# The loop over images of a Mamba layer, written out

## The chip, the cores and the metric

The kernel runs on one core of a Trainium2 chip. The metric is the device time in microseconds of one execution, taken as the median of several runs. All data is fp32.

## The reference

Two layers work on an input of 8 images, 384 channels, 32 x 32 positions. Each is `x = x + layer(groupnorm(x))`. The first layer is a Mamba block over the 1024 positions of an image, and an MLP:

```
t  = layernorm(tokens)                          # 8 x 1024 x 384
xm, z = split(t @ in_proj_w.T)                  # 768 channels each
xc = silu(causal_conv3(xm) + conv_b)
dt, B, C = split(xc @ x_proj_w.T)               # 24, 16, 16
dt = softplus(dt @ dt_proj_w.T + dt_proj_b)
h[l]  = exp(dt[l] * A) * h[l-1] + dt[l] * xc[l] * B[l]   # 768 channels x 16 states
y  = (sum over the states of h * C + xc * D) * silu(z)
t  = gelu(y @ out_proj_w.T @ mlp_w1.T + mlp_b1) @ mlp_w2.T + mlp_b2
```

The second layer routes each position to two of four experts, each a two-layer perceptron of 384 channels, and adds them up.

## The kernel before, in words

The kernel has four blocks: a set-up (weights, group statistics), the Mamba layer, a gate stage, and the experts. In each block every engine has its own stream of instructions, and the streams are held together by semaphores alone.

The Mamba layer works in *units*: half an image, 512 positions with the channels on the 128 partitions, so 16 units. A unit goes through three phases:

- *pre*: group norm and layer norm, in-projection (MU, VAR, XM), convolution, the projections to dt, B and C (XP, CT, DT);
- *scan*: 32 *slots*, one for each of 16 states and each of two groups of three channel blocks. In a slot GpSimd forms the input product `vv` (L475), ScalarE three exponentials (L485), VectorE three scans along the positions (L513); TensorE transposes the result (L544), and VectorE multiplies it by C and adds it to `yy` in four instructions (L531, or L529 in the first two slots);
- *post*: transposes of `yy` (Y, L583), the skip term on VectorE (L590), z (Z, L601), out-projection (O, L639), the MLP (M1, L663; M2, L694), the residual on VectorE (L705, L710) and the statistics for the next layer's norm (L714).

The function `step` writes a *half step*: the scan of one unit, with the post phase of the unit before it and the pre phase of the unit after it. The order of the dense work is written out by hand (`ORDER`, with pads and lags in slots), and shared out over the slots of the scan; VectorE takes at most two dense operations behind each scan. `program` calls `step` for all units. Two half steps (the second half of an image, the first half of the next) are the body of a hardware loop, `eng.Fori(0, NB - 1)` at L1089, of seven iterations. Every engine runs that loop by itself, with a counter in a register, and branches back at its end. One half step without post phase stands before it, one without pre phase behind it.

Waits go through the class `Event`: L111 is its `wait_ge`. A unit's number `unit.n` is `b * 2 + half`; inside the loop `b` is the loop's register, so the value waited for has to be computed by register operations at run time:

```
        eng.wait_ge(self.sem, unit.n * (self.per_unit * self.step)
                    + (self.base + (i + 1 - back * self.per_unit) * self.step))
```

With a plain number it is a constant, and a wait that reaches back before the first unit is left out (`unit.static and unit.n < back`). In the same way tiles and DRAM tensors indexed by the image (`st1` at L714, `gn0` at L725, the loads and stores of `x`) have an address from a register in the loop and a constant one outside. The experts' block has a loop of its own over images (L1533), and the gate stage some small ones.

Of the kernel before, what the change touches and what calls it, by code (L numbers as in the profile page):

```python
# [26 lines left out]
NB, C, L = 8, 384, 1024  # L27
# [212 lines left out]
def layer0(nc, a, sem, psum, ident, st1, gn0, eps, x_d, x1_d, b_d, dt, wu, vv, consts):  # L240
    with ExitStack() as ctx:
# [306 lines left out]
        def exp_table(eng):  # L548

            eng.preload_act_table_set("natural_log_exp_and_others")  # L550
# [533 lines left out]
        def program(eng, name):  # L1084
            if name == "act":
                exp_table(eng)
            step(eng, name, pres=Unit(0, 0))
            step(eng, name, scan=Unit(0, 0), pres=Unit(0, 1))
            with eng.Fori(0, NB - 1) as i:  # L1089
                step(eng, name, scan=Unit(i, 1), posts=Unit(i, 0), pres=Unit(i + 1, 0))  # L1090
                step(eng, name, scan=Unit(i + 1, 0), posts=Unit(i, 1), pres=Unit(i + 1, 1))
            step(eng, name, scan=Unit(NB - 1, 1), posts=Unit(NB - 1, 0))
            step(eng, name, posts=Unit(NB - 1, 1))

        s_const = sem("layer1_constants")
        with nc.Block() as block:
            @block.sync
            def _(eng):
                for event in (e_m1, e_m2, e_bn, e_st, e_yz, e_sz, e_t, e_ge, e_x1):
                    event.prime(eng)  # L1100
                program(eng, "sync")
                e_st.wait(eng, Unit(NB - 1, 1))

            @block.gpsimd
            def _(eng):
                program(eng, "pool")
                last = Unit(NB - 1, 1)
                e_v.wait(eng, last)
                e_scan.wait(eng, last)
                for tile, src in consts.loads:  # L1110
                    eng.dma_start(tile, src).then_inc(s_const, 16)
                eng.wait_ge(s_const, 16 * len(consts.loads))

            @block.scalar
            def _(eng):
                program(eng, "act")

            @block.vector
            def _(eng):
                program(eng, "dve")  # L1120

            @block.tensor
            def _(eng):
                program(eng, "pe")
# [499 lines left out]
```

## Time and profile before

| | us |
|---|---|
| median of 3 runs (4445.4 to 4457.47) | 4446.55 |
| profiled execution: its own time | 4449.6 |
| profiled execution: span | 4447.9 |
| VectorE busy in the span | 3558.9 |
| TensorE busy in the span | 3895.6 |
| ScalarE busy in the span | 2557.5 |
| GpSimd busy in the span | 2453.9 |

The span runs from the first to the last instruction of the profiled execution. The engines' streams overlap, so busy times don't add up. A row of the timeline gives start, duration, engine, line and operation, and in brackets the idle time of the engine before it with what ended it; "issue" is idle time in which the engine waited for nothing that the profile shows. Rows of engines with a q behind the name are instructions that the engine's sequencer handles itself, such as branches, register operations and waits.

### The profile page before, as it was taken

How to read it: one execution, taken by the hardware profiler on the slowest of the kernel's cores; microseconds unless marked ns; L12 is line 12 of the kernel's file. 1: busy time of each engine (PE TensorE's matmuls, PEld its weight loads, DVE VectorE, ACT ScalarE, POOL GpSimd, SP SyncE). 2: the span in 40 equal slices, each digit the busy share in tenths (PEclk: the TensorE clock that was granted, in tenths of full speed). 3: DMA queues.
4: the chain of work that ended last, by engine and by line, in shares of the span. 5: the costliest groups of instructions: out<-in, count | busy, mean ns of one | idle time of the engine just before them, and what ended most of it. 6: DMA issues, size and time to landing. Idle time of an engine off the chain costs nothing. (4 is left out here: it accounts for less than half of the span.)

```text
span 4447.9 us, 55651 instructions
## 1 busy us (share of the span) xinstructions
PE 3895.6 (88%) x15209; PEld 2309.2 (52%) x15209; DVE 3558.9 (80%) x4770; ACT 2557.5 (57%) x3970; POOL 2453.9 (55%) x1172
## 2 busy tenths in 40 slices
PE   4568998989898989888998889898978959999999
PEld 3234444444444444444444444444444438888887
DVE  3699998999899999989998999899998245556554
ACT  2466666666676757676666666676754323434343
POOL 1686777777667777776777777767775110000000
PEclk9679999999999999999999999999989969999999
DMA  4011211121111111221211121111111241112110
GB/s 161 31 40 38 68 46 58 47 68 50 58 52 52 52 59 45 69 66 38 68 47 57 47 68 45 61 54 52 52 49 47 105 145 38 38 38 57 38 38 34
DMA packets 114427, 252.94 MB, mean 57 GB/s; under 512 B 11324, under 2 KB 11708, under 8 KB 113636
## 3 DMA queue, kind: packets, MB, share of 16 engines
q1 hardware_dynamic: 108176, 227.12, 15.4%
q0 software_dynamic: 3920, 17.98, 1.1%
q10 hardware_dynamic: 2052, 4.52, 0.3%
q8 instruction: 127, 2.08, 0.2%
q14 instruction: 152, 1.25, 0.1%
HBM read 223.82 MB, written 25.76 MB: 56 GB/s over the span
## 5 line engine op out<-in xcount | busy, mean ns | idle before, releaser
L475 POOL TENSOR_TENSOR vv<-wu,bb 128x1536 f32<-128x1536 f32 x512 | 1767.0, 3453 | 922.1 <-DVE hh L513 920.4
L485 ACT ACTIVATE bank<-dt,a_neg 128x512 f32<-128x512 f32 x1536 | 1046.4, 689 | 1092.4 <-DVE hh L513 1061.9
L544 PEld LDWEIGHTS bank<-ident,hh 128*128 128x128 f32 x6144 | 783.5, 150 | 1208.3 <-DVE yy L531 520.7
L544 PE MATMUL bank<-ident,hh 128*128 128x128 f32 x6144 | 1067.8, 299 | 306.8 <-DVE yy L531 276.6
L531 DVE SCALAR_TENSOR_TENSOR yy<-bank,ct,yy 128x384 f32<-128x384 f32 x1920 | 1110.9, 597 | 55.2 <-PE bank L544 53.2
L513 DVE TENSOR_TENSOR_SCAN hh<-bank,hl,vv 128x512 f32<-128x512 f32 x768 | 978.6, 1274 | 113.8 <-ACT bank L485 84.2
L513 DVE TENSOR_TENSOR_SCAN hh<-bank,vv 128x512 f32<-128x512 f32 x768 | 930.4, 1212 | 127.8 <-ACT bank L485 94.7
L663 PE MATMUL bank<-tt,wring 128*128 128x512 f32 x1152 | 555.8, 598 | 24.4 <-ACT hid L678 19.9
L694 PE MATMUL bank<-hid,wring 128*128 128x512 f32 x1152 | 550.3, 595 | 7.9 <-ACT hid L678 6.1
L1527 POOL DMA_DIRECT2D out<-xb x16 | 12.3, 766 | 839.3 <-DVE xb L1522 839.3
L1477 ACT ACTIVATE dt<-bank,vv 128x512 f32<-128x512 f32 x192 | 132.2, 689 | 387.0 <-PE bank L1398 386.9
L792 PE MATMUL bank<-xn,w_in 128*128 128x512 f32 x576 | 299.4, 631 | 38.6 <-POOL xn L782 38.4
L639 PE MATMUL bank<-xc,w_out 128*128 128x512 f32 x576 | 293.2, 627 | 0.0
L1496 DVE TENSOR_TENSOR dt<-dt,wu 128x512 f32<-128x512 f32 x192 | 129.7, 689 | 191.5 <-ACT dt L1477 191.5
L601 PE MATMUL bank<-xn,w_in 128*128 128x512 f32 x576 | 273.8, 595 | 5.8 <-DVE xc L590 5.8
L663 PEld LDWEIGHTS bank<-tt,wring 128*128 128x128 f32 x1152 | 193.8, 191 | 150.2 <-issue 123.8
L694 PEld LDWEIGHTS bank<-hid,wring 128*128 128x128 f32 x1152 | 194.6, 191 | 133.3 <-issue 122.5
L825 POOL TENSOR_TENSOR xc<-xc,xm 128x510 f32<-128x510 f32 x192 | 226.2, 1180 | 21.6 <-ACT xc L815 12.9
L1396 PE MATMUL bank<-xg_hi,we_hi 128*128 128x512 f32 x576 | 225.1, 391 | 10.0 <-DVE xg_lo L1412 10.0
L1397 PE MATMUL bank<-xg_lo,we_hi 128*128 128x512 f32 x576 | 224.8, 390 | 0.0
L1398 PE MATMUL bank<-xg_hi,we_lo 128*128 128x512 f32 x576 | 224.8, 390 | 0.0
L1396 PE MATMUL bank<-hb_hi,we_hi 128*128 128x512 f32 x576 | 224.1, 389 | 0.0
(160 smaller groups left out, 4695.5 us busy)
## 6 DMA issues: line engine op xcount, KB each, us to landing
wring<-in_w_m SPq DMA_DIRECT2D x192, 384.0 KB, 3.0
bb<-b_rows SPq DMA_DIRECT2D x256, 256.0 KB, 3.3
xn<-in_x SPq DMA_DIRECT2D x24, 768.0 KB, 4.5
xb<-x_scratch SPq DMA_DIRECT2D x24, 768.0 KB, 4.7
xr<-in_x SPq DMA_DIRECT2D x20, 768.0 KB, 4.9
x_scratch<-xr SPq DMA_DIRECT2D x16, 768.0 KB, 3.8
out<-xb POOLq DMA_DIRECT2D x16, 768.0 KB, 3.9
wu<-top_weights SPq DMA_DIRECT2D x32, 256.0 KB, 4.8
```

Source lines behind the costliest of these rows:

```text
L475: e_v.inc_by(eng.tensor_tensor(vv[:, k % 2, :, :], wu[:, u.half, G3 * g:G3 * g + G3, :], bb[:, n % NBB:n % NBB + 1, :].to_broadcast([P, G3 ...
L485: e_da.inc_by(eng.activation(da[t % NDA][:, :], dt[:, u.half, j, :], ACT.Exp, scale=a_neg[:, j, n:n + 1]))
L513: e_scan.inc_by(eng.tensor_tensor_scan(hh[:, k % 2, i, :], da[(G3 * k + i) % NDA][:, :], vv[:, k % 2, i, :], start, ALU.mult, ALU.add))
L531: ins = eng.scalar_tensor_tensor(out=y, in0=ht[c % NHT][:, 0:G3 * P], scalar=scale, in1=y, op0=ALU.mult, op1=ALU.add)
L544: ins = eng.transpose(ht[c % NHT][:, i * P:(i + 1) * P], hh[:, k % 2, i, c * P:(c + 1) * P], ident[:, :])
L601: ins = eng.matmul(bank("Z", j)[:, :], w, xn[:, u.half, k, :], start=(k == 0), stop=(k == KC - 1))
L639: ins = eng.matmul(bank("O", m)[:, :], w_out[:, k, m * P:(m + 1) * P], xc[:, u.half, k, :], start=(k == 0), stop=(k == KD - 1))
L663: ins = eng.matmul(bank("M1", m)[:, :], w[:, m % 2, k, :], tt[:, k, :], start=(k == 0), stop=(k == KC - 1))
L694: ins = eng.matmul(bank("M2", i)[:, :], w[:, k, :], hid[:, k, :], start=(k == 0), stop=(k == HH - 1))
L792: ins = eng.matmul(bank("XM", j)[:, :], w_in[:, k, j * P:(j + 1) * P], xn[:, v.half, k, :], start=(k == 0), stop=(k == KC - 1))
L825: ins = eng.tensor_tensor(y[:, d:T], y[:, d:T], xm[:, j % 2, tap, 0:T - d], ALU.add)
L1396: eng.matmul(bank, w[0], hi, start=start, stop=False)
```

## The change

The hardware loop over images becomes a loop of the program that writes the kernel: its body is written out seven times, `i` is a plain number, and nothing else is edited. This goes for all five engines.

```diff
--- before.py
+++ after.py
@@ -1086,7 +1086,7 @@
                 exp_table(eng)
             step(eng, name, pres=Unit(0, 0))
             step(eng, name, scan=Unit(0, 0), pres=Unit(0, 1))
-            with eng.Fori(0, NB - 1) as i:
+            for i in range(NB - 1):
                 step(eng, name, scan=Unit(i, 1), posts=Unit(i, 0), pres=Unit(i + 1, 0))
                 step(eng, name, scan=Unit(i + 1, 0), posts=Unit(i, 1), pres=Unit(i + 1, 1))
             step(eng, name, scan=Unit(NB - 1, 1), posts=Unit(NB - 1, 0))
```

With it go the branches of L1089, the register operations of L111 and of the addresses in these seven iterations, and the waits that the first units don't need.

## Rows read from the trace of the kernel before

**Rows 1.** Busy time of each engine in windows, by iteration of the loop.

```profile
334.30:746.40 412.10, 373.21 (x1400) 197.30 (x1400) 381.54 (x487) 276.85 (x429) 299.86 (x143) 0.95 0.16 53
746.40:1164.00 417.60, 374.42 (x1400) 199.24 (x1400) 382.17 (x487) 278.18 (x430) 302.51 (x143) 0.94 0.17 56
```

Columns: window, its length, busy time and instructions of PE, PEld, DVE, ACT and POOL, granted TensorE clock, DMA share, GB/s.

**Rows 2.** VectorE's waits, 746.4 to 1164: total us, times, longest.

```profile
DVE hh L513 <- ACT bank L485: 23.2, 21, 1.7
DVE hh L513 <- issue: 5.0, 1, 5.0
```

**Rows 3.** Line 1089: durations in ns, first and last start.

```profile
L1089 PEldq COMPARE_BRANCH  x7: 76/5983/6502, 745.5 to 3249.0; - x7
L1089 DVEq COMPARE_BRANCH  x7: 55/63/72, 746.4 to 3249.9; - x7
```

**Rows 4.** VectorE's timeline from 3243 to 3271.

```profile
3249.18 1.26 DVE L531 SCALAR_TENSOR_TENSOR yy<-bank,ct,yy 128x384 f32<-128x384 f32 x2 [0.36 <-PE bank L544]
3252.19 1.28 DVE L513 TENSOR_TENSOR_SCAN hh<-bank,hl,vv 128x512 f32<-128x512 f32 x1 [1.76 <-POOL vv L475]
...
3269.04 1.28 DVE L513 TENSOR_TENSOR_SCAN hh<-bank,hl,vv 128x512 f32<-128x512 f32 x1 [0.25 <-ACT bank L485]
```

**Rows 5.** VectorE's timeline around the first and the sixth taken branch.

```profile
745.67 1.28 DVE L531 SCALAR_TENSOR_TENSOR yy<-bank,ct,yy 128x384 f32<-128x384 f32 x2 [0.34 <-PE bank L544]
751.99 1.28 DVE L513 TENSOR_TENSOR_SCAN hh<-bank,hl,vv 128x512 f32<-128x512 f32 x1 [5.04 <-issue]
...
961.02 1.22 DVE L513 TENSOR_TENSOR_SCAN hh<-bank,vv 128x512 f32<-128x512 f32 x1 [1.62 <-POOL vv L475]
...
2832.48 1.26 DVE L531 SCALAR_TENSOR_TENSOR yy<-bank,ct,yy 128x384 f32<-128x384 f32 x2 [0.35 <-PE bank L544]
2837.82 1.28 DVE L513 TENSOR_TENSOR_SCAN hh<-bank,hl,vv 128x512 f32<-128x512 f32 x1 [4.08 <-issue]
...
3047.55 1.22 DVE L513 TENSOR_TENSOR_SCAN hh<-bank,vv 128x512 f32<-128x512 f32 x1 [1.62 <-POOL vv L475]
```

**Rows 6.** GpSimd's timeline at the first taken branch.

```profile
745.45 3.43 POOL L475 TENSOR_TENSOR vv<-wu,bb 128x1536 f32<-128x1536 f32 x1
```

**Rows 7.** VectorE's timeline in the first half of the first iteration.

```profile
334.91 1.28 DVE L513 TENSOR_TENSOR_SCAN hh<-bank,hl,vv 128x512 f32<-128x512 f32 x1
...
352.10 1.28 DVE L513 TENSOR_TENSOR_SCAN hh<-bank,hl,vv 128x512 f32<-128x512 f32 x1 [0.25 <-ACT bank L485]
...
543.88 1.22 DVE L513 TENSOR_TENSOR_SCAN hh<-bank,vv 128x512 f32<-128x512 f32 x1 [1.81 <-POOL vv L475]
```

**Rows 8.** Line 111 on VectorE: first in 334 to 3250, then in 3252 to 3463.

```profile
L111 DVEq ALU_OP  x3745: 40/40/52, 336.3 to 3249.2; - x198
...
L111 DVEq EVENT_SEMAPHORE  x156: 21/21/50, 3256.8 to 3462.4; - x156
```

**Rows 9.** VectorE's timeline: a slot in the loop, a slot behind it.

```profile
500.56 1.27 DVE L513 TENSOR_TENSOR_SCAN hh<-bank,hl,vv 128x512 f32<-128x512 f32 x1
...
506.19 1.28 DVE L513 TENSOR_TENSOR_SCAN hh<-bank,hl,vv 128x512 f32<-128x512 f32 x1
...
3277.89 1.27 DVE L513 TENSOR_TENSOR_SCAN hh<-bank,hl,vv 128x512 f32<-128x512 f32 x1
...
3283.52 1.27 DVE L513 TENSOR_TENSOR_SCAN hh<-bank,hl,vv 128x512 f32<-128x512 f32 x1
```

**Rows 10.** VectorE's timeline: statistics in the loop, then behind it.

```profile
737.93 0.67 DVE L710 TENSOR_TENSOR xr<-xr,bank 128x512 f32<-128x512 f32 x1
738.75 0.69 DVE L714 BATCH_NORM_STATS2 st<-xr 128x512 f32 x1
...
3429.20 0.68 DVE L710 TENSOR_TENSOR xr<-xr,bank 128x512 f32<-128x512 f32 x1
3429.91 0.69 DVE L714 BATCH_NORM_STATS2 st<-xr 128x6 f32<-128x512 f32 x1
```

**Rows 11.** DMA queues from 334 to 746: packets, MB, share of 16 engines.

```profile
q14 instruction: 19, 0.16, 0.1%
```

## The prediction

> **What bounds the kernel now.** I split the time by stages first. The loop over images that the diff rewrites runs seven times and fills 334.3 to about 3250 us of the span; in the windows by iteration [rows 1] the first takes 412.1 us and the second 417.6 us. VectorE is busy 382 us of such an iteration, TensorE 374 us at a granted clock of 0.94, the others far less. The chain that ended last says nothing on this stage: it runs through the second layer's matmuls only. So I took VectorE's waits within an iteration [rows 2]: its scans wait 23.2 us in all for ScalarE's exponentials, 21 times, and once, for 5.0 us, for "issue", that is, for nothing that the profile shows. The same view of the first iteration has the first wait and not the second. This one stands between VectorE's last multiply-accumulate of an iteration and its first scan of the next.
>
> The instructions of line 1089 [rows 3] say what it is. VectorE's branch is issued at 746.4 us and lasts 63 ns, but the next instruction of its stream, the register operation of L1089 at the loop's head, comes only when the 5.0 us of [rows 2] are nearly over; TensorE's branch itself is shown as 5983 ns in the median, up to 6502. Only six of the seven branches on each engine are taken. After the seventh, at 3249.9 us, the stream simply goes on, and VectorE's next scan waits 1.76 us for GpSimd's product and for nothing else [rows 4]. A taken branch costs a reload of the stream; code that runs on doesn't.
>
> **The change, part by part.**
>
> *The reload, on the path.* From the end of the last multiply-accumulate to the first scan of the next half step (the boundary inside the iteration, where no branch is) VectorE takes 745.67 + 1.28 = 746.95 to 961.02, or 214.07 us, around the first taken branch, and 2833.74 to 3047.55, or 213.81 us, around the last [rows 5]; the six lie between 213.81 and 214.26, mean 213.97. What is it without a branch? Two pieces. The boundary: [rows 4] measures it in code without a branch, 1.76 us of idle time. It follows from GpSimd too: at 745.45 us it begins the first product of the new half step, which takes 3.43 us [rows 6], so this is ready at 748.9, and the scan that now begins at 751.99 could begin there, 1.9 us after 746.95. From the first scan to the boundary inside: the first iteration, entered without a branch, takes 334.91 to 543.88, 208.97 us [rows 7]. Of that, 0.34 us belongs to TensorE being only just in time: from the first scan to the ninth's wait for ScalarE it is 17.19 us there, and 16.85 us where VectorE had stood for 1.76 us and TensorE had its transposes ready [rows 4, 7]. In the new kernel TensorE will be early in the same way, so 208.63 us. Sum: 1.76 + 208.63 = 210.39 us for 213.97, 3.58 us less each time, and six times make 21.5 us. The least that this can be is the idle time alone: the six waits are 5.04, 4.34, 4.36, 4.85, 5.11 and 4.08 us (the fifth is put down to GpSimd), 27.8 us, less 6 x 1.76: 17.2 us. I take 21.5 because the remainder is TensorE's 6 us of lateness, which the same branches cause.
>
> The reload on ScalarE, GpSimd and SyncE I cost at nothing. They branch before VectorE does, and their cover is VectorE's tail: GpSimd's product at 745.45 follows its previous work at once [rows 6]. If SyncE's loads of the next weights go out some us earlier, they meet no deadline: at the inner boundary and at the fall-through they do so already, and VectorE's wait there is the 1.6 to 1.8 us for GpSimd.
>
> What is late next: GpSimd, for those 1.76 us, and behind it nothing new; the 23 us for ScalarE per iteration stay.
>
> *The register operations.* VectorE issues 3745 of them in the loop at 40 ns [rows 8], 150 us of its issuing. In code written out they are replaced by waits with constants, which are not free of instructions either: the static step after the loop shows 156 waiting instructions of 21 ns on VectorE. Whether either is exposed is read from the slots: three scans and four multiply-accumulates take 506.19 - 500.56 = 5.63 us inside the loop and 3283.52 - 3277.89 = 5.63 us in the static step [rows 9]. Both streams are issued ahead of the work. So zero; at the rows' resolution of 0.01 us and 64 slots by 7 iterations this could hide 4.5 us either way, which goes into the range.
>
> The Trainium skill, page "Advanced Engine Details and Errata", section "Control Flow Timing", gives a compare-and-branch about 108 ns. By that the whole change would be worth 6 x 0.108, or 0.65 us, and would come out as no change; VectorE's branch row of 63 ns [rows 3] is of its size, TensorE's 5983 is not. Against it stands the page "Runtime: NRT & Kernel Launch", section "Instruction fetch mechanics": a taken branch to code outside the two buffered pages stalls for a fetch.
>
> *Addresses from a register.* The statistics of line 714 write to a tile indexed by the image. Directly behind L710 they start 738.75 - (737.93 + 0.67) = 0.15 us late in the loop, and 3429.91 - (3429.20 + 0.68) = 0.03 us late in the static step [rows 10]. Two of the three in each half step stand so, the other has work between; 28 x 0.12 = 3.4 us, on VectorE and thus on the path. Other such addresses are on DMAs and a small ScalarE copy, both with slack: zero.
>
> *Everything else* (the second layer, the gate, the set-up) has the same instructions. Waits that are dropped because they reach back before the first unit were met from the start.
>
> Sum: 21.5 + 3.4 = 24.9 us, 0.56%. The profiled execution took 4449.6 us (span 4447.9 and 1.7 around it) and would take 4424.7. The median shown is 4446.55, 3.05 below, so 4421.6 us.
>
> **Rivals.**
>
> *Bigger: register work is exposed at waits.* The slots above are those where VectorE runs without a wait. Where an engine has run dry, the next instruction's register operation could stand in the open. Some 33 times per iteration VectorE waits (21 for ScalarE [rows 2], 11 for TensorE, one for GpSimd); with one or two operations of 40 ns each this is 33 x 7 x 0.04 to 0.08 = 9 to 18 us more, and 4403 to 4412 us. For it: nothing measures it directly. Against it: waits of one kind have one length in both codes (the scan after the ninth slot waits 0.25 us for ScalarE at 352.10 and at 3269.04 [rows 4, 7]).
>
> *No measurable change: the stall returns as another wait.* VectorE's stop at the branch lets the others catch up, and without it they are late elsewhere; the gain falls under 13.3 us, to 4434 to 4447. It needs over 11.6 of the 24.9 us, 1.9 us per boundary. For it: TensorE is busy 90% of an iteration and ScalarE's bursts already stop VectorE. Against it: the stretch behind the branch is no shorter after a 5.04 us stop (751.99 to 961.02, 209.03 us) than in the first iteration without one (208.97), so nothing was caught up.
>
> *No measurable change: the 5 us aren't the branch's.* If the stop at the boundary came from something that stays, the burst of loads that SyncE issues there or a late product of GpSimd, only the address term is gained: 3.4 us, 4443 us. For it: one of the six waits is put down to GpSimd. Against it: the seventh boundary has the same work and 1.76 us [rows 4].
>
> The section "Control Flow Timing" of the Trainium skill, cited above, would make it so: its 0.65 us give 4446 us.
>
> *Slower: long code is fetched late.* Straight code must be brought in block after block: the second of the two instruction queues brought 19 packets of 8 KB in the first iteration [rows 11], 133 in seven; that VectorE's are a third of them, some 45, is an estimate. If a block comes late on VectorE, it costs about what the reload costs, 4.4 us of idle time. Six late blocks (26 us) eat the gain, and nine (39.6 us) make it 4461 us, slower by over 0.3%; that is one block in five. Against it: the loop's body is streamed in the same way today, and VectorE shows no wait for "issue" but at the branches.
>
> The Trainium skill's page "Runtime: NRT & Kernel Launch" says of such a crossing that it is "mostly hidden"; that would leave this rival nothing.
>
> **How the numbers follow.** The forecast has 0.76, the bigger gain 0.06, the stall that returns 0.12, the stall that isn't the branch's 0.02, slower 0.04. Within the forecast the time is 4429 at the least gain (17.2 us) and 4417 at 24.9 + 4.5; so 4416 to 4430 with the scatter of the runs. The range takes in more on both sides, from near the first rival to the edge of the second: 4413 to 4434. 0.3%, or 13.3 us, is about what a measurement of this kernel can tell from none. Faster 0.82, same 0.14, slower 0.04.
>
> **What the next profile would show.** Right: no rows of branches at 1089; no wait of VectorE for "issue" at the six boundaries, each a wait of 1.6 to 2.0 us for GpSimd; iterations of about 413.2 us (417.25, the mean of the six counted from VectorE's last accumulate to its next, less 3.58 and 0.48); slots still 5.63 us; no idle 6 us on TensorE ahead of the transposes of L583; L714 0.03 us behind L710. Wrong: slots other than 5.63 us (register work or waiting instructions matter), "issue" waits inside a step (late blocks), or new waits for TensorE or ScalarE behind the boundaries that take back the 3.6 us.

## The result

The changed kernel takes 4435.35 us (median of 6 runs, 4433.1 to 4438.67) beside 4451.31 us for the kernel before in the same session (6 runs): a ratio of 0.9964, 95% interval 0.9951 to 0.9977. It is faster by 16.0 us, 0.36%. The prediction was 24.9 us: 4421.6 us with a range up to 4434, which the time misses by 1.4 us. The sign holds and so does the reload of the stream; the size doesn't, in part because a term that was put at nothing isn't nothing.

The head of the page of the changed kernel:

```profile
span 4437.0 us, 47230 instructions
PE 3907.3 (88%) x15209; PEld 2302.7 (52%) x15209; DVE 3560.7 (80%) x4770; ACT 2556.8 (58%) x3970; POOL 2455.3 (55%) x1172
```

There were 55651 instructions; the work is the same, instruction for instruction, and VectorE's busy time has grown by 1.8 us. VectorE's timeline at the first two boundaries where a branch was taken, the inner boundary between them, and the seventh outer one:

```profile
748.89 1.26 DVE L531 SCALAR_TENSOR_TENSOR yy<-bank,ct,yy 128x384 f32<-128x384 f32 x2 [0.42 <-PE bank L544]
752.04 1.28 DVE L513 TENSOR_TENSOR_SCAN hh<-bank,hl,vv 128x512 f32<-128x512 f32 x1 [1.89 <-POOL vv L475]
...
960.82 1.22 DVE L513 TENSOR_TENSOR_SCAN hh<-bank,vv 128x512 f32<-128x512 f32 x1 [1.56 <-POOL vv L475]
...
1162.63 1.26 DVE L531 SCALAR_TENSOR_TENSOR yy<-bank,ct,yy 128x384 f32<-128x384 f32 x2 [0.42 <-PE bank L544]
1165.79 1.29 DVE L513 TENSOR_TENSOR_SCAN hh<-bank,hl,vv 128x512 f32<-128x512 f32 x1 [1.90 <-POOL vv L475]
...
3238.02 1.29 DVE L513 TENSOR_TENSOR_SCAN hh<-bank,hl,vv 128x512 f32<-128x512 f32 x1 [1.90 <-POOL vv L475]
```

The 5.04 and 4.08 us of [rows 5] are now 1.9 us, and the seventh, where the branch wasn't taken, 1.76 us in [rows 4], waits 1.90 us as well: all seven look alike. The slots and the statistics, which answer to [rows 9] and [rows 10]:

```profile
503.35 1.27 DVE L513 TENSOR_TENSOR_SCAN hh<-bank,hl,vv 128x512 f32<-128x512 f32 x1
...
508.97 1.27 DVE L513 TENSOR_TENSOR_SCAN hh<-bank,hl,vv 128x512 f32<-128x512 f32 x1
...
734.10 0.68 DVE L710 TENSOR_TENSOR xr<-xr,bank 128x512 f32<-128x512 f32 x1
734.82 0.70 DVE L714 BATCH_NORM_STATS2 st<-xr 128x6 f32<-128x512 f32 x1
```

A slot takes 5.62 us, L714 begins 0.04 us behind L710. What VectorE waits for over the loop (334 to 3250 us; total, times, longest), first before, then after:

```profile
DVE hh L513 <- ACT bank L485: 165.8, 149, 1.8
DVE yy L531 <- PE bank L544: 30.1, 71, 1.1
DVE hh L513 <- issue: 22.7, 5, 5.0
DVE hh L513 <- POOL vv L475: 16.7, 8, 5.1
DVE xc L590 <- PE bank L583: 2.0, 4, 0.7
```

```profile
DVE hh L513 <- ACT bank L485: 165.1, 148, 1.8
DVE yy L531 <- PE bank L544: 33.5, 76, 1.0
DVE hh L513 <- POOL vv L475: 24.0, 14, 2.0
DVE yy L529 <- PE bank L544: 0.8, 3, 0.3
```

"Issue" is gone, GpSimd has 7 us more (it was behind the branch all along), and the waits of the accumulates (L531, L529) for TensorE have grown by some 4 us, while those of L590, 2.0 us, are gone. That is a first sight of what is missing. And the register operations of L111 [rows 8] have become waits with constants, 2203 on VectorE in 334 to 3236 us, where the loop had 267 in 334 to 3250 us; TensorE's are shown too:

```profile
L111 DVEq EVENT_SEMAPHORE  x2203: 21/21/50, 334.7 to 3235.6; - x184
L111 PEldq EVENT_SEMAPHORE  x838: 51/51/777, 336.1 to 3234.5; - x168
```

### The profile page after: what moved, and what is told of

Its sections match the earlier page's. It is cut to its first block and busy times, and to the rows that moved or that the text cites. A ratio compares the mean times of both kernels' runs of the same rounds, so it can differ in the third digit from the quotient of the medians.

```text
span 4437.0 us, 47230 instructions
## 1 busy us (share of the span) xinstructions
PE 3907.3 (88%) x15209; PEld 2302.7 (52%) x15209; DVE 3560.7 (80%) x4770; ACT 2556.8 (58%) x3970; POOL 2455.3 (55%) x1172
## 5 line engine op out<-in xcount | busy, mean ns | idle before, releaser
L531 DVE SCALAR_TENSOR_TENSOR yy<-bank,ct,yy 128x384 f32<-128x384 f32 x1920 | 1113.1, 598 | 63.4 <-PE bank L544 59.5
```

What stands on the lines that cost most here:

```text
L531: ins = eng.scalar_tensor_tensor(out=y, in0=ht[c % NHT][:, 0:G3 * P], scalar=scale, in1=y, op0=ALU.mult, op1=ALU.add)
```

## How the experiments are read

Some effects here are of 3 us, below what the times tell. So besides the time I read three lengths from VectorE's timeline of each profile: the *head*, up to its first scan of the loop's first iteration; the *stretch*, from there to its first scan behind the seventh outer boundary (in [rows 7] and [rows 4], 334.91 to 3252.19, 2917.3 us); and the *tail*, from there to the end of the span. Each kernel ran against the kernel before on the same chip, and the ratio compares these two.

| kernel | median us | ratio, 95% interval | head | stretch | tail |
|---|---|---|---|---|---|
| before, first profile | 4451.31 | | 334.9 | 2917.3 | 1195.7 |
| before_again | 4453.45 | 1.0003, 0.9993 to 1.0012 | 337.2 | 2916.7 | 1194.6 |
| after, first profile | 4435.35 | 0.9964, 0.9951 to 0.9977 | 337.6 | 2900.4 | 1199.0 |
| after_again | 4437.71 | 0.9966, 0.9953 to 0.9978 | 336.9 | 2900.1 | 1198.7 |
| one_trip_loops | 4434.24 | 0.9959, 0.9945 to 0.9973 | 334.8 | 2901.2 | 1194.4 |
| dve_alone | 4454.81 | 1.0005, 0.9996 to 1.0014 | 334.6 | 2917.3 | 1196.1 |
| pe_alone | 4452.72 | 0.9997, 0.9989 to 1.0006 | 335.8 | 2916.7 | 1199.0 |
| dve_and_pe | 4433.78 | 0.9956, 0.9943 to 0.9969 | 336.4 | 2897.1 | 1198.1 |
| three_images_a_pass | 4439.87 | 0.9967, 0.9955 to 0.9979 | 335.5 | 2903.6 | 1192.8 |
| two_images_a_pass | 4442.23 | 0.9973, 0.9964 to 0.9982 | 334.7 | 2910.4 | 1192.7 |
| first_product_early | 4414.25 | 0.9911, 0.9897 to 0.9925 | 338.3 | 2880.6 | 1197.7 |
| product_early_in_loop | 4442.97 | 0.9975, 0.9966 to 0.9985 | 336.0 | 2906.5 | 1194.4 |
| product_early_two_written | 4416.9 | 0.9914, 0.99 to 0.9927 | 336.5 | 2883.0 | 1198.6 |

## The experiments

**Both kernels once more** (no edit).

> The changed kernel once more, for its interval and for a second profile. Theory A (the first profiles differ outside the loop by chance): the stretch before VectorE's first scan of the first iteration (334.9 us before, 337.6 after) and the one behind the last scan boundary (1195.7 before, 1199.0 after) vary between executions of one kernel by some 3 us, and this run lies within 2 us of the kernel before in both; ratio 0.996 to 0.997. Theory B (long code costs something outside the loop too): both stretches are again 2 to 4 us longer than before.

> The kernel before under a new label, for a second profile and the scatter. Ratio 1.000 within 0.002. Six stops of 4 to 5 us for issue at the same six boundaries. If theory A of the run of the changed kernel is right, the stretches outside the loop differ between the two profiles of the kernel before by 1 to 3 us too; if B, they agree within 0.5 us.

The stretch repeats to 0.6 us and is worth 16.8 us (2917.0 to 2900.2). The head differs by 2.2 us between two profiles of the same kernel, so it tells nothing: theory A there. The tail doesn't fit it: two profiles of a kernel agree within 1.2 us, and after is 3.7 us longer than before, as theory B had it. But one_trip_loops, whose code is as long, has the short tail of before, and pe_alone a long one; over all thirteen it varies from 1192.7 to 1199.0 us. The tail has two parts. Up to the last L714 of the Mamba layer it takes 315.4 to 316.4 us in the six profiles in which VectorE's and TensorE's streams run through all seven iterations with constants (one_trip_loops is one of them), and 313.8 to 314.3 us in the seven others, so these 1 to 2 us do come with the writing out. The second layer takes 878.5 to 884.9 us and follows nothing that was changed. What sets either stays open.

**Seven loops of one pass.**

```diff
-            with eng.Fori(0, NB - 1) as i:
+            for n in range(NB - 1):
+                with eng.Fori(n, n + 1) as i:
```

> Seven hardware loops of one pass each instead of one of seven: the code is as long as in the changed kernel, every register operation and register address stays, and no branch is taken. Theory A (the taken branches are the whole effect): the waits for issue at the boundaries go, each is 1.8 to 2.1 us for GpSimd, L714 stays 0.15 us behind L710, and the time is that of the changed kernel, 13 to 18 us below before. Rival (register work has its own share): at least 5 us of the gain is missing, and slots of VectorE take longer than in the changed kernel.

As fast as the changed kernel. But it had 47335 instructions, 105 more than it, not the 55651 of the loop: the register values were known and had been replaced by constants. So it shows a second time that code without a taken branch gives the gain, and nothing of register work.

**One engine's stream written out.** `step` is the same for all; only how its calls are repeated depends on the engine.

```diff
+            if name in ("dve",):        # ("pe",) and ("dve", "pe") in the two below
+                for i in range(NB - 1):
+                    images(i)
+            else:
+                with eng.Fori(0, NB - 1) as i:
+                    images(i)
```

> Only VectorE's stream is written out; the four others loop as before. Theory A (TensorE's reload of 6 us lies beside VectorE's and is as late by itself): VectorE's first scan behind the branch comes at once when GpSimd's product is ready, after 1.9 us instead of 4.6, but its next instruction, L590, then waits 3 to 4 us for TensorE's transposes of L583, and under 1 us of each 3.2 is gained: 0 to 6 us in all. Rival (each engine's reload costs by itself, VectorE's is the one that was seen): 14 to 18 us gained, as by the whole change.

No gain at all, within theory A's 0 to 6 us. VectorE's timeline at the first outer boundary, and TensorE's:

```profile
748.83 1.28 DVE L513 TENSOR_TENSOR_SCAN hh<-bank,hl,vv 128x512 f32<-128x512 f32 x1 [1.89 <-POOL vv L475]
753.25 1.60 DVE L590 SCALAR_TENSOR_TENSOR xc<-xc,d_sk,bank 128x512 f32<-128x512 f32 x2 [3.14 <-PE bank L583]
```

```profile
743.64 2.58 PE L544 MATMUL bank<-ident,hh 128*128 128x128 f32 x9
752.10 4.31 PE L583 MATMUL bank<-ident,yy 128*128 128x128 f32 x19 [5.89 <-issue]
```

The first scan is 3 us earlier and the next instruction waits 3.14 us for TensorE, whose stop of 6 us began almost at the same time. At the six outer boundaries this wait is 1.8 to 3.1 us.

> Only TensorE's stream is written out. Theory A (two reloads lie side by side, VectorE's is the one that stops the scans, TensorE's makes the transposes late behind it): VectorE's stops for issue of 4 to 5 us stay, the waits of L590 for TensorE behind them (0.3 to 0.7 us) go and the stretch from the first scan to the boundary inside shrinks by 0.4 to 0.9 us; 2 to 5 us in all, of the 16.8 us that the loop gained by the whole change. Rival (each engine's part adds up, VectorE's alone was worth nothing so TensorE's is the whole): 14 to 17 us.

No gain either, less than the 2 to 5 us that theory A expected: the waits of L590 went, but the six stops of VectorE grew from 4.63 to 4.92 us in the mean.

> VectorE's and TensorE's streams are written out, the other three loop. Theory A: the whole gain of the loop, 14 to 17 us, since the reloads of ScalarE, GpSimd and SyncE are covered; from VectorE's first scan of the loop to its last boundary 2900 to 2903 us, where the kernel before has 2917. Rival (a third reload comes next, ScalarE's 3.4 us): boundaries with waits for ScalarE of 2 to 3 us, and 5 us or more of the gain missing.

The whole gain, and 3 us less of stretch than the changed kernel; 2.3 us of these are in the second halves, none of which is one of the long ones of 205 us that are described below. The two reloads lie beside each other and hide each other; either alone moves the stretch by 0.3 us, both together by 20. (dve_alone pays some 3 us for its waits with constants besides, as shown below.) The reloads of ScalarE, GpSimd and SyncE are covered, as the prediction had costed them.

**Fewer branches, registers kept.**

```diff
-            with eng.Fori(0, NB - 1) as i:
+            with eng.Fori(0, 2) as n:       # two images: Fori(0, 3), and n * 2 + m
+                for m in range(3):
+                    i = n * 3 + m
...
+            for i in range(NB - 2, NB - 1):
```

> The hardware loop has two passes of three images each, and the seventh image is written out: one taken branch instead of six, with the register operations kept in six of seven iterations (the loops of one pass had lost theirs, so they told nothing of them). The stretch from VectorE's first scan of the loop to its last boundary is 2917 us before and 2900 in the changed kernel. Theory A (a taken branch costs 3.3 us, register operations and constant waits nothing): 2917 - 5 x 3.26 = 2900.7 us. Theory C (where an engine has run dry, the constant waits cost TensorE and VectorE more than register ones, some 0.3 us per half step, which is part of what my sum missed): 2895 to 2898 us, below the changed kernel although one branch is left; second halves of an iteration 203.0 us as before, not 203.3. Theory D (register operations cost): 2904 us or more.

One stop for issue is left, of 6.2 us, and it is at the branch:

```profile
1581.41 1.28 DVE L513 TENSOR_TENSOR_SCAN hh<-bank,hl,vv 128x512 f32<-128x512 f32 x1 [6.24 <-issue]
```

The stretch is 2903.6 us, between A and D, and outside C. Theory C is right for the second halves (from the inner boundary to the last accumulate): 203.1 us in the mean of the six with registers, where the changed kernel's have 203.4 (its one of 205.0, explained below, left out). But four outer boundaries without a branch wait 2.06 to 2.25 us for GpSimd, where constants have 1.9, and the one stop that is left is longer than any in the kernel before, so the total isn't lower.

> Three passes of two images and the seventh image written out: two taken branches. The stretch is 2917 us with six, 2903.6 with one, 2900.2 with none. Theory (each taken branch costs the same 2.8 to 3.5 us, and nothing else of the loop matters): 2905 to 2908 us, with two stops for issue of 4 to 6 us. Rival (what matters is that there is a loop with registers at all, or a jump over a longer way costs more): 2903 us or less, or 2910 us and more.

2910.4 us, 2 to 5 above the theory's and inside the rival's. The stops for the two branches are 5.63 and 5.35 us. Three of its second halves take 204.8 to 205.0 us instead of 203.0, which makes 5.6 us; the kernel before and the changed one have one such each. With one it would be some 2907, which is the theory's; that is a subtraction, not a run. What these are is seen in the changed kernel, in its windows at such a half and then at the same place of an ordinary one (columns as in [rows 1], the clock is the third from the end):

```profile
1405.00:1410.00 5.00, 3.20 (x13) 2.38 (x14) 5.00 (x7) 4.32 (x8) 4.99 (x3) 0.50 0.07 25
1410.00:1415.00 5.00, 5.00 (x12) 2.66 (x12) 4.73 (x7) 4.60 (x6) 5.00 (x3) 0.53 0.02 5
...
991.00:996.00 5.00, 3.19 (x13) 2.28 (x14) 5.00 (x7) 4.24 (x8) 5.00 (x3) 0.55 0.08 24
996.00:1001.00 5.00, 5.00 (x17) 2.64 (x16) 4.65 (x7) 4.67 (x7) 5.00 (x3) 0.77 0.00 0
```

TensorE comes out of a stretch in which it was busy 3.2 of 5 us at 1.2 GHz (0.50). In the next 5 us, fully busy, it stands at 0.53 in the one and 0.77 in the other, so it goes back to 2.4 GHz some us later and VectorE waits 0.8 us more for it here; a second place in the same half gives another 1.0 us. What makes it go back earlier or later isn't shown.

**GpSimd's product earlier.** What the changed kernel has left at its boundaries is the wait for the next unit's first product. It needs only the first three channel blocks, yet stands in GpSimd's order behind the work of all six.

```diff
-                if name == "pool" and live:
+                if name == "pool" and live and k:
                     scan_pool(eng, scan, k)
...
                     for f in at[k]:
+                        if name == "pool" and pres and f is st[("DT", 3)][1]["pool"][1]:
+                            scan_pool(eng, pres, 0)
                         f(eng)
```

> The changed kernel with GpSimd's order altered: the first input product of the next unit's scan is issued ahead of the last three softplus sums (DT3 to DT5) instead of behind them. It goes for what is left at the boundaries, 1.9 and 1.5 us of VectorE waiting for this product. Theory (the product binds there, and TensorE's transposes come next, as at the entry of the loop before): the waits fall under 0.2 us, 0.34 us of each comes back behind them, 14 x 1.35 = 19 us less than the changed kernel, about 4418 us beside a before of 4452. Rival (the later softplus sums or slot 1's product are late instead): waits for GpSimd or ScalarE of over 1 us at the second to fourth scan, and less than 8 us gained on the changed kernel.

4414.25 us beside 4454.09: faster than before by 0.89% (interval 0.75 to 1.03%), 19.7 us of stretch below the changed kernel where the theory had 19, and the fastest of all. GpSimd's timeline, then VectorE's, at the first outer boundary:

```profile
742.34 3.45 POOL L475 TENSOR_TENSOR vv<-wu,bb 128x1536 f32<-128x1536 f32 x1 [0.73 <-POOL wu L917]
```

```profile
749.63 1.26 DVE L531 SCALAR_TENSOR_TENSOR yy<-bank,ct,yy 128x384 f32<-128x384 f32 x2 [0.43 <-PE bank L544]
750.80 1.27 DVE L513 TENSOR_TENSOR_SCAN hh<-bank,hl,vv 128x512 f32<-128x512 f32 x1
752.10 1.60 DVE L590 SCALAR_TENSOR_TENSOR xc<-xc,d_sk,bank 128x512 f32<-128x512 f32 x2
```

The product is ready at 745.8, VectorE goes from its last accumulate into the first scan without a stop, and L590 comes 1.30 us behind the scan's start, 0.1 late.

> GpSimd's early product in the kernel before, with its hardware loop. In the changed kernel it took 19.7 us off VectorE's stretch from the first scan of the loop to the last boundary (2900.2 to 2880.6). Theory A (at an outer boundary the reload of VectorE's stream hides the late product): it can only gain at the seven inner boundaries and the seventh outer one, which isn't branched over; the six stops for issue stay between 4 and 5.5 us; 2917 - 8 x 1.4 = about 2906 us, 11 us less. Rival (the two waits add up): 2897 us, as in the changed kernel.

2906.5 us for a forecast of 2906: the same edit is worth 10.6 us with the hardware loop and 19.7 without. Its waits of VectorE over the loop:

```profile
DVE hh L513 <- issue: 27.1, 6, 4.9
DVE xc L590 <- PE bank L583: 3.5, 10, 0.9
```

The six stops are there in full, and none for GpSimd anywhere: behind a reload that stays, an early product is worth nothing.

> GpSimd's early product with only VectorE's and TensorE's streams written out. Theory C (constant waits on ScalarE, GpSimd and SyncE cost a little): 2 to 4 us less than the early product with all five streams written out (2880.6 us in the stretch), as the two streams written out alone had 2897.1 beside 2900.2; 2877 to 2879 us. Rival (now that GpSimd's product isn't waited for, the reloads of ScalarE and GpSimd come onto the path): waits for ScalarE or GpSimd of 1 us and more at the six outer boundaries, 2885 us or more.

2883.0 us, in neither range. At four of the six outer boundaries VectorE waits 0.5 to 1.5 us, so the other engines' reloads do show now that nothing else is waited for. In time it is the same as with all five written out.

## Why the prediction missed

By its own steps, with the means of two profiles each:

| step | predicted us | measured us |
|---|---|---|
| idle time at six outer boundaries | -17.2 | -16.4 |
| first halves (TensorE early; L714) | -6.0 | -3.2 |
| second halves (L714; register work zero) | -1.7 | +2.7 |
| seventh outer boundary | 0 | +0.1 |
| sum, the stretch | -24.9 | -16.8 |
| head and tail | 0 | +1.2, +3.7 |

Of the 8.1 us that the stretch falls short, 4.4 are in the second halves, 2.8 in the first, and 0.9 at the boundaries.

**The reload: right.** 27.8 us of idle time became 11.4. The pair of single-engine runs shows both parts, VectorE's own stop and TensorE's stop of 6 us beside it. The rival of a stop that isn't the branch's is out: no wait for issue is left in the loop. Late blocks of the size that the other rival needed, 4.4 us, are out with it; small ones may be there, see below.

What the reload waits for is seen in part in the DMA queues of the kernel before: first from 746.4, the branch of VectorE, to 748.9, then from 748.9 to 752 (queue, packets, MB, share of 16 engines).

```profile
q1 hardware_dynamic: 377, 1.00, 101.4%
```

```profile
q1 hardware_dynamic: 89, 0.22, 19.9%
q8 instruction: 1, 0.02, 2.0%
q14 instruction: 2, 0.02, 1.2%
```

In the first 2.5 us no packet of the two instruction queues (q8, q14) starts, while SyncE's loads (q1) fill the DMA engines; the first comes 2.4 to 2.9 us behind VectorE's branch at each of the six. Where the loads last longer the stop does too: they keep the engines busy until 2.5 to 3 us behind the branch in this profile (stops of 4.1 to 5.1 us), until 4.5 to 5 in two_images_a_pass (5.35 and 5.63), and until 5.5 in three_images_a_pass (6.24). So part of what is called the reload may be waiting behind these loads. No run moves the loads, so how the 4 to 6 us divide isn't shown.

**TensorE early: right at the place, lost afterwards.** Over the first three scans behind the six boundaries the changed kernel is 0.34 to 0.99 us ahead of before at five and level at one, 0.59 us in the mean, where the sum had 0.71. Later in the half part of it is gone: of the 0.57 in the second iteration 0.16 is left after 108 us, because VectorE then waits for TensorE where it hadn't; in the mean 0.42 is left. So the second rival, the stall that returns as another wait, was true in part. My row against it (209.03 us after a stop, 208.97 without) compared two halves in which TensorE was late alike and couldn't show it.

**The register operations: this step failed.** "Both streams are issued ahead of the work. So zero" was read from slots in which VectorE never runs dry, and there it holds (5.62 us). Where it waits for TensorE, a wait with a constant costs 0.07 us more than one from a register. three_images_a_pass has both kinds in one kernel. The last accumulate of a second half, first in the sixth iteration (registers), then in the seventh (constants):

```profile
2819.84 1.26 DVE L531 SCALAR_TENSOR_TENSOR yy<-bank,ct,yy 128x384 f32<-128x384 f32 x2 [0.35 <-PE bank L544]
...
3235.86 1.26 DVE L531 SCALAR_TENSOR_TENSOR yy<-bank,ct,yy 128x384 f32<-128x384 f32 x2 [0.42 <-PE bank L544]
```

The other kernels agree: 0.35 or 0.36 us in most second halves where VectorE's waits come from registers (both profiles of before, pe_alone, product_early_in_loop), 0.42 or 0.43 where they are constants. dve_alone has constants on VectorE and the loop on the four others, and its seven second halves take 2.4 us more than before's, although L714 gives back some 0.8 in them: 3.1 us that the sum had put at zero. In the changed kernel they take 2.7 us more. I had looked for the opposite sign in the first rival. How a constant wait comes to be slower there, whether by its place as an instruction of its own or otherwise, isn't shown.

Not all of the 3.1 us are the kind of wait. In dve_alone an accumulate of the second half, first in the sixth iteration, then in the seventh:

```profile
2798.15 1.22 DVE L513 TENSOR_TENSOR_SCAN hh<-bank,vv 128x512 f32<-128x512 f32 x1
2799.28 0.60 DVE L531 SCALAR_TENSOR_TENSOR yy<-bank,ct,yy 128x384 f32<-128x384 f32 x1
...
3214.45 1.22 DVE L513 TENSOR_TENSOR_SCAN hh<-bank,vv 128x512 f32<-128x512 f32 x1
3215.93 0.62 DVE L531 SCALAR_TENSOR_TENSOR yy<-bank,ct,yy 128x384 f32<-128x384 f32 x1 [0.25 <-PE bank L544]
```

L531 comes 1.13 us after the scan's start in six iterations and 1.47 in the seventh, with the same constant waits and TensorE's transposes equally early (0.52 us behind the scan). The seventh iteration of three_images_a_pass has constants too and 1.13 us. So this step belongs to a place in the code. All six profiles with VectorE's stream written out have three such steps of 0.32 to 0.35 us (one of them once 0.20), at the same records of that stream (counted from 0, the sequencer's included: 3519, 3647 and 6463, which are 128 and 22 x 128 apart). In one_trip_loops two stand at 5695 and 6335, again multiples of 128 from there. A packet of the second instruction queue has 8 KB (19 of them make 0.16 MB in [rows 11]), so the steps may be blocks of straight code that come late, the last rival on a small scale. That is argued from the spacing and not shown. Two of the three lie open in second halves, some 0.6 us; the third ends in a shorter wait for GpSimd.

**L714: right at the row, oversized in the sum.** The pairs moved closer by 0.11 us, but in each half the last scan then waits as much as 0.1 us longer for ScalarE, so about 1.5 of the 3.4 us arrive.

**Outside the loop** I had put zero. Two profiles each say 1.2 us for the head, which is less than its scatter, and 3.7 us for the tail; 2 us of that lie before the end of the Mamba layer, in code that is the same in both, and come back in every profile with both engines' streams written out. Their cause is open. The times themselves, 16.0 us and an interval of 10 to 22, can't separate it.

Of the two pages of the Trainium skill that the prediction weighed, "Runtime: NRT & Kernel Launch", section "Instruction fetch mechanics", describes what is seen: a stall behind a taken branch, and none of that size in streamed code. "Advanced Engine Details and Errata", section "Control Flow Timing", agrees with the 55 to 72 ns of VectorE's branch row in order of size, but the 4 to 6 us behind it decide.

## What to carry to other kernels

A taken branch at the end of a long loop body cost VectorE a stop of 4 to 6 us here and TensorE one of 6. A short body doesn't show it. In the same trace the experts' loop (L1533) has 434 matmuls per pass, where the loop over images has 1400 [rows 1]; its branches on TensorE take 208 ns in the median, and TensorE is busy without a gap across them:

```profile
L1533 PEldq COMPARE_BRANCH  x6: 76/208/208, 3848.3 to 4337.9; - x6
```

The DMA engines are idle at the first of these branches (share 0.00), so whether the length of the body or the missing loads make it short, no run separates.

Look whether the engines branch at the same moment: then removing one engine's branch shows nothing, and only the set that lies side by side pays. Look too whether a burst of loads is under way at the branch. A second wait under the reload (here a product 1.9 us late) can be had only after it. Price a change of the kind of wait at places where the engine runs dry, not in the steady state.

## What wasn't expected of the hardware

- With only VectorE's or only TensorE's stream written out the time doesn't move (ratios 1.0005 and 0.9997), with both it falls by 0.44%.
- Where VectorE waits for TensorE, a wait with a constant starts the accumulate 0.07 us later than one with a computed value (0.42 for 0.35 us of idle time), though each register operation takes 40 ns.
- In straight code a few places cost VectorE 0.32 to 0.35 us once, at records of its stream that are multiples of 128 apart.
- Behind VectorE's taken branch no instruction packet starts for 2.4 to 2.9 us, while SyncE's loads fill the DMA engines.
- The granted clock of TensorE goes back to 2.4 GHz (0.50 to 1.00) some us earlier or later at the same place of different iterations, and each late return costs VectorE about 1 us. The long half that comes of it was in the third iteration in both profiles of the changed kernel, in the sixth and in the fifth in those of the kernel before.
- Code that is the same and runs after the loop takes 1192.7 to 1199.0 us in the thirteen profiles, with up to 1.2 us between two profiles of one kernel.
